# A graph kernel's gathers: a small memset in front of each, and fewer waits of GpSimd on TensorE

## What is computed

```python
h = relu(layernorm(x))
# layer 0
h = (h @ W.T).reshape(N, 8, 16)
e = leaky_relu(a_src[src] + a_dst[dst])          # per edge and head
p = exp(e - segment_max(e, dst)[dst])
x = x + segment_sum(p / segment_sum(p, dst)[dst] * h[src], dst) + bias
# layer 1
h = relu(layernorm(x)); q, k, v = h @ Wq + bq, h @ Wk + bk, h @ Wv + bv
score = (q[dst] * k[src]).sum(-1) / 4 + edge_attr @ We + be
p = exp(score - segment_max(score, dst)[dst])
out = segment_sum(p / (segment_sum(p, dst)[dst] + 1e-8) * v[src], dst) @ Wo + bo
x = x + layernorm(out + h) * gamma + beta
```

## Time and profile before

| | us |
|---|---|
| median of 3 runs (1582.59 to 1594.63) | 1584.45 |
| profiled execution, span | 1585.9 |
| TensorE busy | 1020.5 |
| VectorE busy | 934.6 |
| GpSimd busy | 883.4 |
| ScalarE busy | 640.0 |

### The profile page before, as it was taken

The page is one execution under the profiler, slowest core; times in us unless marked ns, Lnnn a source line. Parts: engine busy times, 40 slices in busy tenths (PEclk is TensorE's granted clock), DMA queues, the critical chain, the costliest instruction groups (busy, mean ns, idle before and its releaser), DMA issues.

```text
span 1585.9 us, 21105 instructions
## 1 busy us (share of the span) xinstructions
PE 1020.5 (64%) x4985; PEld 863.7 (54%) x4985; DVE 934.6 (59%) x3002; ACT 640.0 (40%) x1699; POOL 883.4 (56%) x926
## 2 busy tenths in 40 slices
PE   5456666666665766666554577666766676676765
PEld 4345555555554555445354466565655566566664
DVE  6445656556565565557813455656565656656578
ACT  5524334243342433422554234444443434344414
POOL 5766666666666566551046566656666565666500
PEclk9655555555656565566766666877777777777676
DMA  6321222222222222222133222222222222232201
GB/s 138 72 66 43 66 46 66 48 63 45 67 47 67 45 65 47 58 84 57 49 94 95 73 84 84 84 80 80 84 84 84 80 82 81 84 88 83 80 1 41
DMA packets 54202, 110.35 MB, mean 70 GB/s; under 512 B 16876, under 2 KB 30848, under 8 KB 53956
## 3 DMA queue, kind: packets, MB, share of 16 engines
q0 software_dynamic: 36288, 91.12, 22.6%
q1 hardware_dynamic: 16483, 17.39, 4.0%
q10 hardware_dynamic: 1313, 0.50, 0.1%
HBM read 100.60 MB, written 8.81 MB: 69 GB/s over the span
## 4 chain that ended last, share of the span: by engine, by line
DVE 16%; PE 16%; another core or an unknown queue 10%; issue 9%; ACT 2%; DVEq 2%
PE bank L865 6%; PE bank L849 6%; DVE acc L1441 4%; DVE PV L1418 3%; DVE prod L1238 2%; PE bank L836 1%; PE bank L912 1%; DVE raw L1247 1%; DVE halves L1087 1%; PE bank L900 1%; DVEq L1441 1%; ACT S L636 1%; DVEq L1220 0%; DVEq L90 0%
## 5 line engine op out<-in xcount | busy, mean ns | idle before, releaser
L532 POOL DMA_INDIRECT G<-table,idx_all x880 | 857.1, 974 | 544.5 <-issue 280.3
L865 PE MATMUL bank<-PV,S 128*125 128x144 f32 x1760 | 449.5, 416 | 209.5 <-DVE acc L1441 104.4
L865 PEld LDWEIGHTS bank<-PV,S 128*125 128x125 f32 x1760 | 373.9, 287 | 236.1 <-issue 134.9
L1441 DVE TENSOR_TENSOR acc<-acc,bank 125x144 f32 x880 | 260.4, 296 | 339.3 <-remote 191.7
L636 ACT ACTIVATE S<-iota_n,lid 128x125 f32<-128x125 f32 x880 | 275.7, 386 | 0.7 <-issue 0.7
L849 PE MATMUL bank<-qe,ST 125*128 x880 | 182.0, 378 | 87.3 <-DVE prod L1238 80.7
L849 PEld LDWEIGHTS bank<-qe,ST 125*128 125x128 f32 x880 | 164.1, 279 | 96.7 <-issue 95.8
L1418 DVE TENSOR_TENSOR PV<-G,PV 128x512 f32<-128x512 f32 x220 | 151.2, 688 | 23.4 <-issue 22.8
L646 ACT ACTIVATE ST<-bank 125x512 f32<-125x512 f32 x110 | 63.6, 598 | 248.4 <-remote 197.6
L640 ACT ACTIVATE S<-S,ones 128x500 f32<-128x500 f32 x220 | 156.6, 712 | 7.3
L836 PE MATMUL bank<-ident,S 128*125 128x128 f32 x440 | 89.8, 340 | 52.5 <-ACT S L640 31.9
(11 more groups left out here) (219 smaller groups left out, 1093.8 us busy)
## 6 DMA issues: line engine op xcount, KB each, us to landing
G<-table,idx_all POOLq DMA_INDIRECT x880
prod<-in_edge_attr_dram SPq DMA_DIRECT2D x8, 672.0 KB
table<-G SPq DMA_DIRECT2D x12, 224.0 KB
bias_rows<-qe SPq DMA_DIRECT2D x1, 1664.0 KB
table<-h0b SPq DMA_DIRECT2D x8, 178.5 KB
out_dram<-G SPq DMA_DIRECT2D x8, 168.0 KB
prod<-in_edge_attr_dram SPq DMA_DIRECT2D x8, 90.0 KB
xs<-in_x_dram SPq DMA_DIRECT2D x1, 504.0 KB
```

The lines of the kernel that those rows point to most:

```text
L532: pool.indirect_dma_start(G[:, u, v, 0:w], None, table, bass.IndirectOffsetOnAxis(ap=idx_all[:, g * GV + v:g * GV + v + 1], axis=0)).then_ ...
L865: last = pe.matmul(sums_bank(p)[0:BN, at:at + H * SLOT], S[:, ur, v, :], PV[:, v, :, :].rearrange("p h k -> p (h k)"), start=True, stop=True)
L1441: ve.tensor_tensor(a, a, o, ALU.add).then_inc(s.sem["acc_added"], 1)
```

## The change

In front of every one of the 880 gathers GpSimd clears the first 260 columns of the one partition of `pad_i`, which is the whole tensor, and raises a semaphore of its own; each such memset waits for the one before it. And `pace` returns at once for every visit but the ninth of a group (`v == 8`), so that its waits ahead of the 1st, 5th and 13th gather are gone. In group 0 no wait of `pace` is left.

```diff
+        s_space = sem("spacer_set")
...
             def pace(n, g, v):
 
                 s, r, q = L[n], g - UNROLL, g - 1
-                if v % 4:
+                if v != 8:
                     return
...
+            spaces = [0]
+
+            def space(width):
+
+                wait(pool, s_space, spaces[0])
+                pool.memset(pad_i[0:1, :, :].rearrange("p a b -> p (a b)")[:, 0:width], 0).then_inc(s_space, 1)
+                spaces[0] += 1
+
             def gathers(n, table, w):
...
                         for v in range(QV * j, QV * j + QV):
                             pace(n, g, v)
+                            space(260)
                             pool.indirect_dma_start(
```

## The result

The changed kernel takes 1616.84 us, median of four runs (1607.04 to 1623.70), against 1588.51 us for the kernel before (1582.59 to 1594.63): a ratio of 1.0149, with a 95% interval of 1.0102 to 1.0196. It is slower; 1551 was forecast.

The account below looks back on a forecast made before the run. No engine is full; TensorE's counts come late while gathers are issued. With GpSimd the bound at 675.0 us per layer, 1585.9 - 4.7 - 28.3, less 1.45 for the median, gives 1551; likeliest range 1520 to 1568, whole range up to 1640.

Parts of the forecast that it names:

- The reading of what bounds the kernel: Both gather loops: while gathers are issued end to end, TensorE's counts reach other engines late, costing each step some microseconds.
- the waits that go: GpSimd's waits ahead of 1st, 5th and 13th gathers: removal frees 53 us of GpSimd time over 25 first-layer steps.
- The memset's cure: Between gathers: a gap of 0.56 us instead of 0.30 lets TensorE's counts through, shortening steps until GpSimd is the bound.
- The memset's price: Ahead of every gather on GpSimd: 260 columns add 0.26 us, bounds 0 to 0.36, making the spacing 1.534 us.
- The spacing of 1.50 to 1.58 us: Sign of the forecast: starts of L532's gathers with the memset between; about 1.25 would show C, over 1.6 B's price.
- each stretch 675 us, bound by GpSimd: Gather stretch of each layer: 440 gathers at 1.534 us; -4.7 us in the first layer, -28.3 in the second.
- Rival B: First layer: the pause was needed, the spacer does not replace it; above 1600 us, 1647 with one step in four; chance 0.27.
- Rival A: Both gather stretches: the step keeps its length, GpSimd's 24.5 us hide in 24.7 and 25.6; 1585 us; chance 0.28.
- C: Ahead of gathers: memset hides in the 0.30 us gap, gathers keep 1.25 us; 1600 or more, or about 1530; chance 0.05.

## Why the prediction was wrong

**The reading of what bounds the kernel was right in kind.** "TensorE's counts reach the others late while gathers are issued, and pauses let them through" is shown for the late condition: 1236 us and no late wait without gathers; 1740 us and waits of 13.86 us without the pauses. The condition costs 245 us in all, 4.5 us a step; that it could be absent, and the kernel before then take 1343 us, nothing in the one trace told. One reading of it was off: the ten records of the earlier trace rows are two batches, and the third batch's count was seen 4.0 us after its last matmul, not 2.6.

**The step that failed is the price of "the waits that go".** The forecast costed their removal as 53 us of GpSimd time gained, and at no loss, on the ground that the memset's wider gap does the pauses' work. Alone their removal costs 150 us (9.5%), 138 of it in layer 0's stretch; the memsets then give back 123 (1740 to 1617). Beside the memsets it still costs: 1616.84 for the change against 1566.56 with all waits, 2.6% by the two ratios. By the spans that is 48.4 us, of which layer 0 is 22.7, layer 1 16.1, the part between 8.3. So the change is the sum of a gain of 1.1% by the memsets and a larger loss by the waits.

**The memset's cure was right in sign and overrated.** Alone it was to shorten the steps until GpSimd sets them. With all waits it gave 17.0 us in layer 1 and nothing in layer 0. Counts get through oftener, not always: VectorE waited 3.56 us for the carried maxima in the earlier trace rows; the changed kernel's longest such wait is 9.0 us (below, whole program), though in layer 1's median they now come 1.07 us after the start of their matmuls, where it was 2.9.

```profile
DVE CCM L1358 <- remote: 47.7, 9, 9.0
```

**The memset's price, a term of the sum, was mis-sized.** 0.26 us was taken from memsets one behind another, 0 to 0.36 kept as bounds; it is 0.165. The spacing of 1.50 to 1.58 us that was to show the forecast was 1.42. Going by the starts rather than the spans, as the Trainium skill asks in "Perfetto Trace Analysis", section "GPSIMD Engine Instruction", was right: the span says 0.30. But the spacing of memset after memset isn't that of memset and gather. This size isn't what made the forecast wrong: with 1.42 in the sum it would have ended at 1451, further off. 440 x 1.42 = 625 us is far below the 703.8 and 702.4 measured, so the forecast's "each stretch 675 us, bound by GpSimd" fell by its other step.

**Rival B was the right one**, with no memset exactly at the place it named: the third batch's count, raised just ahead of a group's first gather, is out until the ninth's wait (13.86 us of waiting at 490.73). In the changed kernel that count comes through, and others, raised two gathers later, stay out in its place (6.30 and 10.96 us of waiting at 475.82 and 477.94). Its price, 1647 or more, was for pauses gone and no help from the memset at all; the runs give 1740 for just that, and 1617 with the help. The forecast and B were thus not alternatives but two terms of one sum, +150 and -123, and I had given each a chance instead of adding them. The terms depend on each other: taken the other way round they are -19 for the memsets with all waits kept, and +50 for the waits then lost.

**Rival A** had beside it the sentence of the Trainium skill, "SBUF — State Buffer", section "Who interferes with whom", that DMA never contends with a compute engine. Gathers on GpSimd turned 1236 us into 1585 with late counts; with prompt ones, 1233 into 1339. The page speaks of SBUF ports, and in those terms the traces agree for VectorE and ScalarE, whose busy times are within 1% with gathers and without (934.6 and 926.3 us, 640.0 and 634.7). TensorE's is 1020.5 against 937.5 us, at a mean granted clock of 0.666 against 0.727; what made it longer is not shown. What is delayed is the count, on which that section says nothing.

**C** is out: the memset does not hide wholly in the gap (1.42 against 1.25 us).

## What to carry to other kernels

A wait that protects no data can still carry time as a pause; before it is taken out, ask what else gets through while the engine stands, and cost the removal and its substitute as two terms, each with a run of its own, and both together. Before work is added to an issuing engine, compare its work a step with the step in the kernel's best condition, not in the one profiled: here 22.7 us hid in steps of 25 and cost 9% in steps of 21. And compare with the kernel before on the same chip at the same time; the same edit was worth nothing in one condition and 9.5% or 15% in the other.

## What was unexpected of the hardware

- The same program took about 1344 us at one time and 1585 to 1590 a quarter or half an hour later, on the same chips. What differs is the waits for TensorE's counts, and up to 60 us of TensorE's busy time; it needs the gathers to show (1233 and 1236 us without them). The late trace also lacks more than a quarter of VectorE's and ScalarE's semaphore events.
- With late counts a count of TensorE was not seen through nine gathers in a row, 11.0 us, and then 1.5 us after the last.
- In that condition a memset of 2 or 130 columns between gathers makes the kernel slower (by 15 and 13% with the ninth's wait, where no memset costs 9.5%, and 130 columns by 4.9% with all waits) and one of 260 makes it faster. It isn't explained.
- GpSimd's idle time ahead of a gather is 0.30 us behind a gather, in either condition, 0.21 to 0.23 behind a memset of 2 columns and 0.16 behind one of 130 or 260.
